# Dense products of a two-layer graph network with the weight blocks as the stationary operand

## Chip, cores and metric

One core of one Trainium2 chip. The metric is the device time of one execution in microseconds (us), the median over runs. Engines are named as the profile names them: PE (TensorE matmuls), PEld (its weight loads), DVE (VectorE), ACT (ScalarE), POOL (GpSimd), SP (SyncE, which here only issues DMAs).

## What is computed

96 nodes with 1024 features each, 1632 edges, two layers. All of it is float32. The reference, cut to what matters:

```python
h = relu(layernorm(x))                                  # 96 x 1024
q = h @ wq.T + bq;  k = h @ wk.T + bk;  v = h @ wv.T + bv
q2 = q @ wiq.T + biq;  k2 = k @ wik.T + bik;  v2 = v @ wiv.T + biv    # 16 heads of 64
attn = softmax(q2 @ k2.T / 8 + mask)                    # mask from the edges and their types
x = x + (attn @ v2) @ wo.T + bo
h = relu(layernorm(x))
u = h @ root + bias
for r in range(8):                                      # mean of h over each node's edges of type r
    u = u + mean_r(h) @ weight[r]
z = concat(u, h) @ w_gate + b_gate
x = x + tanh(u) * z + h * (1 - z)
```

That is 18 products of 96x1024 by 1024x1024: WQ, WK, WIQ, WIK, WV, WIV, WO, ROOT, eight relations and the two halves of the gate. Their weights are 72 MB and are read once.

## The kernel before

The host lays every 1024x1024 weight matrix out as four **pieces** of 1 MB: a half of the input features (four blocks of 128 on the partitions) by a half of the output features (512 columns). 72 pieces run in one fixed order.

The path of a piece: SP fetches it into one of eight slots of `raw` (L260 to L270, where slots are refilled when `split` says that the piece has been read). ACT rounds it to fp32r into `high` (`round_piece`, L413), DVE takes the rest, `raw - high`, into `low` (`split_piece`, L589); both have four slots. PE then makes, for each of the four blocks, three matmuls (`multiply`, L848 to L850): the stationary operand is a 128x96 block of the activations, high or low part, and 512 columns of the weights move past it.

```python
pe.matmul(o, stat[0][:, at], hi, start=opens and k == 0, stop=False)
pe.matmul(o, stat[1][:, at], hi, start=False, stop=False)
mm = pe.matmul(o, stat[0][:, at], lo, start=False, ...)
```

So a piece is 12 matmuls and its output has the nodes on the partitions (96x512, `acc`). The bias comes in as one more matmul for each half of a product (L861). Before such an output can be the input of the next product, it is turned: ACT copies it to `rows` (`take_rows`, L422), PE transposes four 128-wide blocks (`turn_rows`, L890) into `turn`, ACT rounds that (`take_turned`, L426), DVE takes its low part (`low_turned`, L599 or L602).

Beside the products stands the work on edges and attention: keys of the edges compared with each other (L906, L630), one-hot matrices made by POOL (L328, L354) and DVE (L648, L673), codes of the mask (L920) and counts by type (L933, 32 matmuls with 384 columns moving), scores (L950), softmax, attention transposed (L961), values mixed (L974), sums of messages (L1080, L1081) and their means (L794). Every engine's order is written out by hand; the 32 pieces of the relations run in a loop over pairs of relations (ACT, DVE and PE each have one), with the sums of the next pair inside it. The result is made by DVE (L832, L833) and stored in two halves.

Of the kernel before, what the change touches and what calls it, by code (L numbers as in the profile page):

```python
# [18 lines left out]

WQ, WK, WIQ, WIK, WV, WIV, WO, ROOT, REL0 = range(9)
PIECES = 4
RAW_SLOTS = 8  # L40
SPLIT_SLOTS = 4
# [5 lines left out]
TURNED = ["h0", "q", "k", "q2", "k2", "v", "out", "h1", "u"]  # L47

SPLIT_TURNED = ["h0", "q", "k", "v", "out", "h1", "u"]


def gnn_kernel(nc, x, weights, biases, edge_columns, edge_rows, type_weights, out):
# [4 lines left out]
    M = weights.shape[0] // PIECES  # L57
    R = M - REL0 - 2
# [9 lines left out]
    WG_X, WG_U = REL0 + R, REL0 + R + 1  # L68
    N_PIECES = PIECES * M
    FIRST_REL = PIECES * REL0  # L70
    FIRST_GATE = PIECES * WG_X
    TW = N * CH
    NB = biases.shape[0]
    LOW_ROW = 32
    ROUNDS = N_PIECES // RAW_SLOTS
    assert D == 1024 and N % 32 == 0 and N <= P and R % 2 == 0 and EC == 16 and EP <= P
    assert N_PIECES % RAW_SLOTS == 0 and FIRST_REL % RAW_SLOTS == 0

    with ExitStack() as ctx:
# [5 lines left out]


        raw = sb("raw", [P, RAW_SLOTS, CH * HALF])
        high = sb("high", [P, SPLIT_SLOTS, CH * HALF], F32R)
        low = sb("low", [P, SPLIT_SLOTS, CH * HALF], F32R)
        x_sb = sb("x_sb", [N, D])  # L90
        rows = [sb(f"rows{i}", [N, D]) for i in range(2)]
        v2 = sb("v2", [P, D])

        stat_h = [sb(f"stat_h_{s}", [P, C * N], F32R) for s in ("high", "low")]
        stat_a = [sb(f"stat_a_{s}", [P, C * N], F32R) for s in ("high", "low")]
        stat_b = [sb(f"stat_b_{s}", [P, C * N], F32R) for s in ("high", "low")]
        q2T = sb("q2T", [P, E // 2])
        k2T = sb("k2T", [P, C * N])
        attn = sb("attn", [P, E])
        attnT = sb("attnT", [P, HEADS * N])  # L100
# [3 lines left out]
        bias_rows = sb("bias_rows", [LOW_ROW + NB, D], F32R)  # L104
        bias_pick = sb("bias_pick", [LOW_ROW + NB, NB], F32R)
        bias_pick_f = sb("bias_pick_f", [LOW_ROW + NB, NB])
        per_count = sb("per_count", [P, R * N])
# [13 lines left out]
        node_iota = sb("node_iota", [EP, R * N], F16)  # L121
# [6 lines left out]
        code_m = sb("code_m", [N, 2, N])  # L128


        def inside(t, parts, first, shape, dt):

            n = int(np.prod(shape))
            flat = t[:, :] if dt == F32 else t[:, :].bitcast(dt)
# [1021 lines left out]
```

## Time and profile before

| | |
|---|---|
| median of 3 runs | 280.95 us (280.81 to 281.11) |
| span of the profiled execution | 280.8 us |
| PE, PEld busy | 247.4 us (88%), 169.8 us (60%) |
| DVE, ACT, POOL busy | 227.9 us (81%), 171.9 us (61%), 106.6 us (38%) |
| read from HBM | 76.01 MB, 272 GB/s over the span |
| chain that ended last | PE 72%, POOL 13%, DVE 9% |

The profile is one execution; its span is within 0.2 us of the median. A busy share counts the records of an engine, and the records of matmuls overlap: each lasts from its issue to the end of its way through the array. For what a matmul costs in a stream, the distance from one start to the next is read, not the mean duration. The page of the profile has the span in 40 slices; PEclk there is the granted clock of TensorE as a share of full speed (2.4 GHz; 0.5 is 1.2 GHz).

### The profile page before, as it was taken

How to read it: one execution, taken by the hardware profiler on the slowest of the kernel's cores; microseconds unless marked ns; L12 is line 12 of the kernel's file. 1: busy time of each engine (PE TensorE's matmuls, PEld its weight loads, DVE VectorE, ACT ScalarE, POOL GpSimd, SP SyncE). 2: the span in 40 equal slices, each digit the busy share in tenths (PEclk: the TensorE clock that was granted, in tenths of full speed). 3: DMA queues.
4: the chain of work that ended last, by engine and by line, in shares of the span. 5: the costliest groups of instructions: out<-in, count | busy, mean ns of one | idle time of the engine just before them, and what ended most of it. 6: DMA issues, size and time to landing. Idle time of an engine off the chain costs nothing.

```text
span 280.8 us, 3219 instructions
## 1 busy us (share of the span) xinstructions
PE 247.4 (88%) x1144; PEld 169.8 (60%) x1144; DVE 227.9 (81%) x154; ACT 171.9 (61%) x133; POOL 106.6 (38%) x79
## 2 busy tenths in 40 slices
PE   0499556999999979869589999999999999999994
PEld 0266333667666647546357667667766766666662
DVE  2599299797866979996593999999899899974992
ACT  4699703366658588635532975686686677765730
POOL 4999789593795652000100430450322044000000
PEclk9999956899999999979959999999999999999999
DMA  6999978758777764885716489999989999980001
GB/s 196 382 424 423 423 296 332 289 188 279 293 289 268 240 243 149 299 300 177 272 42 259 159 327 398 376 338 357 404 316 371 364 322 328 361 364 0 0 0 56
DMA packets 10974, 76.54 MB, mean 273 GB/s; under 512 B 1440, under 2 KB 1440, under 8 KB 1748
## 3 DMA queue, kind: packets, MB, share of 16 engines
q1 hardware_dynamic: 10964, 76.40, 72.8%
q8 instruction: 7, 0.11, 0.2%
q14 instruction: 3, 0.02, 0.0%
HBM read 76.01 MB, written 0.39 MB: 272 GB/s over the span
## 4 chain that ended last, share of the span: by engine, by line
PE 72%; POOL 13%; DVE 9%; ACT 2%; DMA 1%; issue 1%; POOLq 0%
PE acc L848 22%; PE acc L850 21%; PE acc L849 21%; POOL attn L328 7%; DVE low L589 5%; POOL attn L346 2%; PE side L933 2%; PE acc L861 2%; DVE per_count L747 1%; DMA x_sb<-in_x 1%; PE turn L890 1%; POOL edge_tmp L343 1%; PE turn L1080 1%; DVE edge_tmp L654 1%; ACT high L413 1%
## 5 line engine op out<-in xcount | busy, mean ns | idle before, releaser
L589 DVE TENSOR_TENSOR low<-raw,high 128x2048 fp32r<-128x2048 f32 x72 | 176.5, 2473 | 20.9 <-ACT high L413 20.8
L413 ACT ACTIVATE high<-raw 128x2048 fp32r<-128x2048 f32 x72 | 136.9, 1911 | 33.5 <-PE acc L850 29.5
L848 PE MATMUL acc<-high,stat_h_high 128*96 128x512 f32 x80 | 36.0, 450 | 10.9 <-DVE low L589 10.2
L848 PE MATMUL acc<-high,stat_a_high 128*96 128x512 f32 x112 | 45.1, 403 | 0.0
L850 PE MATMUL acc<-low,stat_a_high 128*96 128x512 f32 x112 | 44.2, 395 | 0.0
L849 PE MATMUL acc<-high,stat_a_low 128*96 128x512 f32 x112 | 43.9, 392 | 0.0
L848 PE MATMUL acc<-high,stat_b_high 128*96 128x512 f32 x96 | 39.0, 407 | 2.3 <-DVE stat_b_low L602 2.3
L850 PE MATMUL acc<-low,stat_b_high 128*96 128x512 f32 x96 | 38.6, 402 | 0.0
L849 PE MATMUL acc<-high,stat_b_low 128*96 128x512 f32 x96 | 38.3, 399 | 0.0
L849 PE MATMUL acc<-high,stat_h_low 128*96 128x512 f32 x80 | 34.5, 431 | 0.0
L850 PE MATMUL acc<-low,stat_h_high 128*96 128x512 f32 x80 | 34.4, 430 | 0.0
L398 POOL TENSOR_TENSOR stat_a_low<-attnT,stat_a_high 128x768 fp32r<-128x768 f32 x4 | 11.8, 2957 | 54.6 <-ACT stat_a_high L538 54.6
L848 PEld LDWEIGHTS acc<-high,stat_h_high 128*96 128x96 f32 x80 | 14.5, 182 | 18.2 <-DVE low L589 6.4
L848 PEld LDWEIGHTS acc<-high,stat_a_high 128*96 128x96 f32 x112 | 18.1, 161 | 8.3 <-issue 0.5
L850 PEld LDWEIGHTS acc<-low,stat_a_high 128*96 128x96 f32 x112 | 18.1, 161 | 7.8
L849 PEld LDWEIGHTS acc<-high,stat_a_low 128*96 128x96 f32 x112 | 18.1, 162 | 7.2
L354 POOL TENSOR_SCALAR attnT<-node_iota,edge_tmp 102x768 f16<-102x768 f16 x4 | 18.4, 4592 | 10.0 <-PE side L933 10.0
L848 PEld LDWEIGHTS acc<-high,stat_b_high 128*96 128x96 f32 x96 | 15.9, 165 | 9.1 <-DVE stat_b_low L602 2.4
L328 POOL TENSOR_SCALAR attn<-node_iota,edge_f 102x96 f16<-102x96 f16 x16 | 20.9, 1327 | 0.0
L398 POOL TENSOR_TENSOR stat_b_low<-attnT,stat_b_high 128x768 fp32r<-128x768 f32 x4 | 13.1, 3285 | 17.9 <-ACT stat_b_high L538 17.9
L850 PEld LDWEIGHTS acc<-low,stat_b_high 128*96 128x96 f32 x96 | 15.7, 164 | 6.8
L849 PEld LDWEIGHTS acc<-high,stat_b_low 128*96 128x96 f32 x96 | 15.9, 166 | 6.4
(130 smaller groups left out, 248.4 us busy)
## 6 DMA issues: line engine op xcount, KB each, us to landing
raw<-in_weights SPq DMA_DIRECT2D x72, 1024.0 KB, 6.6
x_sb<-in_x SPq DMA_DIRECT2D x1, 384.0 KB, 3.7
out<-rows SPq DMA_DIRECT2D x2, 192.0 KB, 2.1
rows<-in_biases SPq DMA_DIRECT2D x2, 36.0 KB
edge_i<-in_edge_columns SPq DMA_DIRECT2D x1, 25.5 KB
attn<-in_edge_rows SPq DMA_DIRECT2D x1, 12.8 KB
tw_in<-in_type_weights SPq DMA_DIRECT2D x1, 1.5 KB, 7.1
```

What stands on the lines that cost most here:

```text
L328: gp.tensor_scalar(src_hot[:, c, :], node_iota[:, 0:N], src_f[:, c:c + 1], None, ALU.is_equal).then_inc(src_hot_ready, 1)
L343: step(gp.tensor_scalar(zero_f, dup_f, 0.0, None, ALU.is_equal))
L346: gp.tensor_tensor(dst_hot, dst_hot, code_e.rearrange("p (c a) -> p c a", a=1).to_broadcast([EP, EC, N]), ALU.mult).then_inc(dst_hot_ready, 1)
L354: gp.tensor_scalar(rel_hot[:, c % 4, :], node_iota[:, :], rel_key_f[:, c:c + 1], None, ALU.is_equal).then_inc(rel_hot_gp, 1)
L398: gp.tensor_tensor(chunks(s[1]), mean[:, :, parity * N:(parity + 1) * N], chunks(s[0]).bitcast(F32), ALU.subtract).then_inc(mean_low, 1)
L413: act.activation(high[:, slot % SPLIT_SLOTS, :], raw[:, slot, :], ACT.Copy)\
L589: dve.tensor_tensor(low[:, s, :], raw[:, slot, :], high[:, s, :].bitcast(F32), ALU.subtract).then_inc(split, 1)
L848: pe.matmul(o, stat[0][:, at], hi, start=opens and k == 0, stop=False)
L849: pe.matmul(o, stat[1][:, at], hi, start=False, stop=False)
L850: mm = pe.matmul(o, stat[0][:, at], lo, start=False, stop=last and kind % 2 == 1 and k == CH - 1 and bias is None)
L861: return pe.matmul(acc[m % 2][0:N, b, :], bias_pick[:, m:m + 1].to_broadcast([LOW_ROW + NB, N]), bias_rows[:, b * HALF:(b + 1) * HALF], st ...
L933: mm = pe.matmul(side[0:N, b, 0:TW], src_hot[:, c, :], rel_hot[:, c % 4, b * TW:(b + 1) * TW], start=c == 0, stop=c == EC - 1)
```

## The change

Every product is turned round. The stationary operand is now a 128x128 block of the float32 weights, read from the slot into which the DMA wrote it. The activations move past it: 96 columns, one for each node, with the features on the partitions. A piece is 16 matmuls of plain float32. Its output has output features on the partitions, the form in which the next product wants it. With that:

- no `high` and `low` of weights or activations; `round_piece`, `split_piece`, `take_rows`, `take_turned`, `low_turned` are gone; 12 slots instead of 8, freed by PE itself (`piece_used`), fetched by a plain loop without a hardware loop (L256 to L262 there)
- the order of the matrices puts the gate's half that takes h (WG_X) ahead of the relations, and the order of the pieces of a matrix is first input half for both output halves, then second
- a product is taken by one DVE addition of the bias for each half (`take`, L410), the bias being per partition; no bias matmuls
- x is turned at the start (L607), the residual stays turned, v2 (L614, L682), the second layer's rows (L614) and the result (L614, L583, L584) are turned back
- one-hot matrices all on DVE, the attention's subtraction and scaling too; the counts use a table of 16 one-hot matrices and stand behind WIV and WO
- sums of messages by block of 128 features for all 8 relations (32 matmuls of 128x384 instead of 64 of 128x192), placed among the pieces of ROOT and WG_X; means of all relations are kept (24 KB per partition)

```diff
-            def multiply(n, slot, kind, stat, a, opens, last, bias=None):
-                b, k0 = kind // 2, CH * (kind % 2)
-                pe.wait_ge(split, n + 1)
-                for k in range(CH):
-                    hi = high[:, slot % SPLIT_SLOTS, k * HALF:(k + 1) * HALF]
-                    lo = low[:, slot % SPLIT_SLOTS, k * HALF:(k + 1) * HALF]
-                    at = slice((k0 + k) * N, (k0 + k + 1) * N)
-                    o = a[0:N, b, :]
-                    pe.matmul(o, stat[0][:, at], hi, start=opens and k == 0, stop=False)
-                    pe.matmul(o, stat[1][:, at], hi, start=False, stop=False)
-                    mm = pe.matmul(o, stat[0][:, at], lo, start=False,
...
+            def piece(n, moving, a, opens=True, closes=True):
+                s, kind = n % SLOTS, KINDS[n % PIECES]
+                b, k0 = kind // 2, CH * (kind % 2)
+                pe.wait_ge(raw_landed[s], 16 * (n // SLOTS + 1))
+                for c in range(CH):
+                    for k in range(CH):
+                        at = k * HALF + c * P
+                        mm = pe.matmul(a[:, b, c * N:(c + 1) * N], raw[:, s, at:at + P],
+                                       moving(k0 + k), start=opens and k0 == 0 and c == 0 and k == 0,
+                                       stop=closes and k0 > 0 and c == CH - 1 and k == CH - 1)
+                mm.then_inc(piece_used, 1)
...
-                act.activation(high[:, slot % SPLIT_SLOTS, :], raw[:, slot, :], ACT.Copy)\
-                   .then_inc(rounded, 1)
...
-                dve.tensor_tensor(low[:, s, :], raw[:, slot, :], high[:, s, :].bitcast(F32),
-                                  ALU.subtract).then_inc(split, 1)
...
+            def take(m, b, dst, bias):
+                dve.wait_ge(piece_used, done_at(m, b))
+                a = acc[1 if SEQUENCE.index(m) % 2 or m >= ROOT else 0]
+                dve.tensor_tensor(by_chunk(half(dst, b)), by_chunk(bank(a, b)), bias_of(bias, b),
+                                  ALU.add).then_inc(taken, 1)
...
+            for b in range(2):
+                pe.wait_ge(taken, taken_at(WO, b))
+                turn_columns(turn, b, xT, rows_turned)
+                for c in ((5, 6) if b == 0 else range(7, EC)):
+                    count(c)
+            pe.wait_ge(normed, 3)
+            turn_rows(turn, 0, rows, h_turned)
...
+            for r in range(R):
+                n = first_piece(REL0 + r)
+                for j in range(PIECES):
+                    if r == 0 and j % 2 == 0:
+                        pe.wait_ge(mean_ready, C if j == 0 else 2 * C)
+                    piece(n + j, of_mean(r), acc[1], opens=False, closes=r == R - 1)
```

What that makes of PE's order, first at WIQ and WIK. Before, two pieces of WIQ's 24 matmuls look so (the first rows of a piece, then the end of one with the turning of the product before it and the counts):

```order
L848 MATMUL acc<-high,stat_a_high 96x512
L849 MATMUL acc<-high,stat_a_low 96x512
L850 MATMUL acc<-low,stat_a_high 96x512
L861 MATMUL acc<-bias_rows,bias_pick 96x512
L890 MATMUL turn<-ident,rows 128x96 x4
L933 MATMUL side<-attnT,attn 96x384 x4
```

Now, WK to the first piece of WV, 16 matmuls to a piece:

```order
L596 MATMUL acc<-hT,raw 128x96 x96
L596 MATMUL acc<-qT,raw 128x96 x32
L638 MATMUL side<-dst_hot,src_hot 96x96 x8
L638 MATMUL turn<-dst_hot,src_hot 96x96 x8
L596 MATMUL acc<-qT,raw 128x96 x32
L596 MATMUL acc<-kT,raw 128x96 x64
L596 MATMUL acc<-hT,raw 128x96 x16
L659 MATMUL side<-k2T,q2T 96x96 x8
```

Three matmuls of 512 columns for a block have become four of 96 columns, nothing is turned between the products, and the counts have moved behind WIV.

PE between the layers, from WO to ROOT. Before, the end of WO, the turning of h and the first of ROOT:

```order
L850 MATMUL acc<-low,stat_b_high 96x512
L861 MATMUL acc<-bias_rows,bias_pick 96x512
L890 MATMUL turn<-ident,rows 128x96 x8
L848 MATMUL acc<-high,stat_h_high 96x512
L849 MATMUL acc<-high,stat_h_low 96x512
```

Now:

```order
L596 MATMUL acc<-hT,raw 128x96 x48
L614 MATMUL turn<-ident,xT 96x128 x4
L647 MATMUL side<-mean,src_hot 96x384 x4
L614 MATMUL turn<-ident,xT 96x128 x4
L647 MATMUL side<-mean,src_hot 96x384 x18
L607 MATMUL turn<-ident,rows 128x96 x4
L596 MATMUL acc<-hT,raw 128x96 x16
L607 MATMUL turn<-ident,rows 128x96 x4
L596 MATMUL acc<-hT,raw 128x96 x16
L798 MATMUL side<-counts,ones 128x384 x2
```

The residual's rows are turned back before the statistics, and 22 of the 32 matmuls of the counts fill the place where PE waits for the normalisation.

DVE at the end of layer 0 (WIK to WO). Before, with the low parts among the steps of the softmax:

```order
L713 SCALAR_TENSOR_TENSOR attn<-side,mask 96x384 x2
L719 TENSOR_REDUCE row_max<-attn 96x8
L589 TENSOR_TENSOR low<-raw,high 128x2048
L602 TENSOR_TENSOR stat_a_low<-turn,stat_a_high 128x384
L726 TENSOR_REDUCE row_sum<-attn 96x8
L729 RECIPROCAL row_inv<-row_sum 96x8
L589 TENSOR_TENSOR low<-raw,high 128x2048
```

Now:

```order
L512 SCALAR_TENSOR_TENSOR attn<-turn,mask 96x384 x2
L518 TENSOR_REDUCE row_max<-attn 96x8
L521 TENSOR_TENSOR attn<-attn,row_max 96x768
L410 TENSOR_TENSOR qT<-acc,bias_cols 128x384
L527 TENSOR_REDUCE row_sum<-attn 96x8
L528 RECIPROCAL row_inv<-row_sum 96x8
L530 TENSOR_TENSOR attn<-attn,row_inv 96x768
L410 TENSOR_TENSOR qT<-acc,bias_cols 128x384
```

The 72 long subtractions are gone, and two steps of the softmax have come over from POOL.

## Rows read from the trace of the kernel before

**Rows 1.** Page: span, busy times, chain that ended last.

```profile
span 280.8 us, 3219 instructions
PE 247.4 (88%) x1144; PEld 169.8 (60%) x1144; DVE 227.9 (81%) x154; ACT 171.9 (61%) x133; POOL 106.6 (38%) x79
...
PE 72%; POOL 13%; DVE 9%; ACT 2%; DMA 1%; issue 1%; POOLq 0%
```

**Rows 2.** Page: DVE's and ACT's costliest groups (line, engine, operation, count | busy, mean ns | idle before).

```profile
L589 DVE TENSOR_TENSOR low<-raw,high 128x2048 fp32r<-128x2048 f32 x72 | 176.5, 2473 | 20.9 <-ACT high L413 20.8
L413 ACT ACTIVATE high<-raw 128x2048 fp32r<-128x2048 f32 x72 | 136.9, 1911 | 33.5 <-PE acc L850 29.5
```

**Rows 3.** Timeline, PE: successive matmuls of a piece (start us, duration us, what).

```profile
68.30 0.40 PE L850 MATMUL acc<-low,stat_a_high 128*96 128x512 f32 x1
68.53 0.39 PE L848 MATMUL acc<-high,stat_a_high 128*96 128x512 f32 x1
```

**Rows 4.** Windows: stretch, engines' busy us and counts, granted clock, DMA share, GB/s.

```profile
20.00:30.00 10.00, 9.76 (x43) 6.21 (x42) 8.56 (x6) 9.92 (x10) 10.00 (x7) 1.00 1.01 423
...
130.00:140.00 10.00, 6.76 (x31) 4.42 (x32) 7.13 (x9) 5.80 (x4) 0.76 (x2) 1.00 0.62 221
```

**Rows 5.** Timeline, PE's weight loads of the message sums (128 columns), second and last.

```profile
150.10 0.19 PEld L1081 LDWEIGHTS turn<-counts,msgs_low 96*128 96x128 f32 x1
...
151.67 0.19 PEld L1081 LDWEIGHTS side<-counts,msgs_low 96*128 96x128 f32 x1
```

**Rows 6.** Timeline, PE: the matmuls of these sums (192 columns), second and last.

```profile
150.19 0.28 PE L1081 MATMUL turn<-counts,msgs_low 96*128 96x192 f32 x1
...
151.76 0.28 PE L1081 MATMUL side<-counts,msgs_low 96*128 96x192 f32 x1
```

**Rows 7.** One line's instructions, L950 (scores): loads and matmuls, min/median/max ns.

```profile
L950 PEld LDWEIGHTS side<-k2T,q2T x32: 156/162/162, 90.2 to 94.8; 64*96 64x96 f32 x32
L950 PE MATMUL side<-k2T,q2T x32: 242/245/320, 90.2 to 94.9; 64*96 64x96 f32 x32
```

**Rows 8.** Timeline, PE: the 16 records of one call of L950.

```profile
90.23 0.92 PE L950 MATMUL side<-k2T,q2T 64*96 64x96 f32 x16
```

**Rows 9.** One line's instructions: loads of L974, L1080 and L890.

```profile
L974 PEld LDWEIGHTS turn<-attnT,v x32: 133/137/137, 114.1 to 119.6; 96*64 96x64 f32 x32
...
L1080 PEld LDWEIGHTS side<-counts,msgs_high x16: 192/192/192, 150.9 to 221.4; 96*128 96x128 f32 x16
...
L890 PEld LDWEIGHTS turn<-ident,rows x64: 137/140/230, 7.6 to 261.7; 96*128 96x128 f32 x64
```

**Rows 10.** Timeline: transposes, eight at 0.5 of the clock, eight at full clock.

```profile
7.65 1.51 PE L890 MATMUL turn<-ident,rows 96*128 96x96 f32 x8 [7.65 <-DVE rows L611]
...
106.62 0.82 PE L961 MATMUL side<-ident,attn 96*96 96x96 f32 x8
```

**Rows 11.** Timeline: the start, to the first product.

```profile
8.56 0.49 ACT L426 ACTIVATE stat_h_high<-turn 128x384 fp32r<-128x384 f32 x1 [1.45 <-PE turn L890]
10.00 1.91 ACT L413 ACTIVATE high<-raw 128x2048 fp32r<-128x2048 f32 x1 [0.30 <-DMA raw<-in_weights]
14.40 0.71 PE L848 MATMUL acc<-high,stat_h_high 128*96 128x512 f32 x1 [3.71 <-DVE low L589]
...
17.74 0.39 PE L850 MATMUL acc<-low,stat_h_high 128*96 128x512 f32 x1
```

**Rows 12.** Chain that ended last in time: four matmuls of the counts (start us, us, what).

```profile
59.63 0.65 PE side L933 x4
```

**Rows 13.** Timeline: between the layers, last statistics and normalisation.

```profile
136.88 0.69 DVE L767 BATCH_NORM_STATS2 stats<-x_sb 96x6 f32<-96x512 f32 x1
...
138.76 1.00 DVE L611 TENSOR_SCALAR rows<-x_sb,moments 96x512 f32<-96x512 f32 x2 [0.95 <-POOL moments L300]
```

**Rows 14.** Timeline, the end: last product, two DVE steps, store.

```profile
276.83 0.69 DVE L832 TENSOR_TENSOR v<-acc,v 96x512 f32<-96x512 f32 x1 [2.36 <-PE acc L850]
...
278.26 0.34 SPq L273 DMA_DIRECT2D out<-rows  x1
```

More of the change, by code:

```diff
@@ L575, in _ @@
+            for b in range(2):
+                act.wait_ge(out_turned, b + 1)
+                act.activation(cols(out_rows, b), turn[0:N, b, :], ACT.Copy).then_inc(out_ready, 1)
         @block.vector
@@ L740, in _ @@
-            invert_sums(1)
+            take(WV, 0, qT, B_V)
+            divide_by_sums(0)
+            take(WV, 1, qT, B_V)
+            divide_by_sums(1)
+            take_both(WIV, kT, B_IV)
+            for b in range(2):
+                dve.wait_ge(piece_used, done_at(WO, b))
+                dve.tensor_tensor(half(xT, b), bank(acc[0], b), half(xT, b), ALU.add).then_inc(taken, 1)
+                dve.wait_ge(rows_turned, b + 1)
+                dve.bn_stats(stats[:, b, :], turn[0:N, b, :]).then_inc(vec, 1)
@@ L1015, in _ @@
[L1015 to L1030 removed]
+            piece(n + 2, of(qT), acc[0])
@@ new lines, in _ @@
+            show_scores(1)
+            piece(n + 2, of(hT), acc[0])
+            piece(n + 3, of(hT), acc[0])
+            n = first_piece(WIV)
+            pe.wait_ge(taken, taken_at(WV, 0))
+            piece(n, of(qT), acc[1])
+            turn_attn(0)
+            piece(n + 1, of(qT), acc[1])
+            pe.wait_ge(taken, taken_at(WV, 1))
+            piece(n + 2, of(qT), acc[1])
+            turn_attn(1)
+            piece(n + 3, of(qT), acc[1])
+            turn_v2(0)
+            for c in range(0, 3):
+                count(c)
@@ new lines, in _, with sum_messages @@
+            pe.wait_ge(normed, 3)
+            turn_rows(turn, 0, rows, h_turned)
+            def sum_messages(c):
+                if c == 0:
+                    pe.wait_ge(msgs_low, 2)
+                    pe.wait_ge(counts_taken, 2)
+                elif c == 1:
+                    pe.wait_ge(totals_taken, 1)
+                else:
+                    pe.wait_ge(mean_ready, 2 * (c - 1))
+                for s in range(2):
+                    for b in range(2):
+                        mm = pe.matmul(bank((turn, side)[c % 2], b), msgs[s][:, c * P:(c + 1) * P], half(counts, b),
+                                       start=s == 0, stop=s == 1)
+                mm.then_inc(sums_shown, 1)
@@ L1066, in _ @@
-            pe.wait_ge(turn_low, low_at("h1", 0))
-            piece(28, stat_h, False)
-            def sum_messages(pair):
-                if isinstance(pair, int) and pair == 0:
-                    pe.wait_ge(msgs_low, 2)
-                else:
-                    pe.wait_ge(mean_ready, pair * 2)
-                pair_counts = counts[:, bass.ds(pair * (2 * N), 2 * N)]
-                for c in range(C):
-                    o = (turn, side)[c // CH][:, (c % CH) // 2, (c % 2) * 2 * N:(c % 2 + 1) * 2 * N]
-                    pe.matmul(o, msgs[0][:, c * P:(c + 1) * P], pair_counts, start=True, stop=False)
-                    mm = pe.matmul(o, msgs[1][:, c * P:(c + 1) * P], pair_counts, start=False, stop=True)
-                mm.then_inc(sums_shown, 1)
@@ L1121 @@
+            n = first_piece(WG_U)
+            for j in range(PIECES):
+                if j % 2 == 0:
+                    pe.wait_ge(taken, taken_at(TAKEN[-1], j // 2))
+                piece(n + j, of(uT), acc[0], opens=False)
+            for b in range(2):
+                pe.wait_ge(out_made, b + 1)
+                turn_columns(turn, b, outT, out_turned)
 def kernel(**inputs):
```

895 lines of the change are left out of this document (313 added, 582 removed).

## Prediction

> **What bounds it now.** I read the page first, then the groups, then PE's timeline. The page has PE busy for 88% of the span, DVE for 81%, and the chain that ended last runs through PE for 72% [rows 1]. PE's busy share doesn't say what it could do, since records of matmuls overlap. In a piece the starts are 0.23 us apart [rows 3]: 512 columns at 2.4 GHz are 0.213 us, so this is nearly full speed. 72 pieces of 12 matmuls at 0.231 us are 200 us, 2.78 a piece, against a span of 280.8. The other 80 us are waits and small work: the head, the low parts on DVE, which cost 2.47 us a piece and wait for ACT's rounding [rows 2], and in layer 0 the edges' work on POOL, 13% of the chain. The first 30 pieces take from 14.4 to 150 us, 4.5 each [rows 11, 5]; the last 42 from 152 to 277, 3.0 each [rows 6, 14]. The DMAs moved 423 GB/s while they had free slots [rows 4], 2.48 us a piece: they are not the limit. So the change may save the distance between 200 and 281 us; what it makes of the 200 decides.
>
> **What a turned product costs.** It removes the 72 roundings and 72 low parts [rows 2], the 18 bias matmuls and the turning between products. It adds 16 plain float32 matmuls a piece. One such matmul makes two records: L950 calls it 16 times and has 32 loads and 32 matmuls [rows 7]. So the pieces are 72 x 16 x 2 = 2304 pairs of load and matmul, where there were 864 pairs.
>
> The matmul of a pair: 16 of L950 with 96 columns take 0.92 us, and the last of them lasts 0.245 [rows 7, 8]. They run two by two, on the upper and lower 64 rows of the array; eight pairs, so one start every (0.92 - 0.245)/8, about 84 ns, on each half. Transposes with 96 columns of float32 agree: eight take 0.82 us [rows 10], less the last one's 0.245 and by seven that is 82 ns. That is 2 x 96 columns at 2.4 GHz (80 ns) and some 3. Hence a pair costs at least 82 ns.
>
> The load of a pair: 64 columns have records of 137 ns, 96 columns 162 [rows 7, 9], 128 columns of fp32r 192 [rows 5, 9]. They lie on one line, some 84 ns plus 0.83 ns a column. A load of 128 columns would then hold the loading path for 107 ns, longer than the matmul. The message sums show it at work: their loads are 128 columns, their matmuls 192 columns of fp32r, which are 80 ns of streaming, just as 96 columns of float32 are. Their loads start at 150.10 and, 14 later, at 151.67 [rows 5], their matmuls at 150.19 and 151.76 [rows 6]: 112 ns a pair, not 82. This is the nearest row that there is to the new pair: same load, same streaming time. What it doesn't show is plain float32 in both, 128 rows instead of 96, and more than 1.8 us of it. The bounds are 82 ns (the load hidden, as in the transposes) and 187 ns (107 + 80, nothing hidden). I take 112, since these loads lie on the line of the plain float32 ones.
>
> A piece is then 32 x 0.1117 = 3.57 us, and 72 are **257.4 us**, 57 more than the 200 of today. The DMA's 2.48 a piece stays hidden behind it, with 12 slots; if PE were at 2.7 it would still be.
>
> The Trainium skill (TensorE: Matmul & The Clock Gate, "Back-to-back issue gap") speaks for less: a sustained stream of loads and matmuls is measured there at some 81 ns a matmul for 128 columns. By it the pieces would be 2304 x 0.081, an estimated 187 us, and the change a clear gain. The row of the message sums, with 112 ns at full clock, contradicts it for 4-byte weights, and I follow the row.
>
> **The rest of the time, all on PE's path.**
> - Head: activations of the first half were ready at 8.56 + 0.49 = 9.05 us [rows 11], and no low part is waited for any more, nor a rounding of the weights. The first piece had landed at 10.0 (ACT's wait for it ends there); now it is issued second in SP's queue, not fourth. Start at 9.4, where the first product stood at 14.40. DVE's added step on x and the bias copy on ACT lie in the wait for the statistics.
> - Clock: the first product's records last 0.71 us at 14.40 and 0.39 at 17.74, some 3.2 us on [rows 11]; till then it ran at half the clock, as the eight transposes did that take 1.51 us at the start and 0.82 later [rows 10]. Half of 3.2: 1.6 us.
> - Small matmuls: counts 32 at 0.163 [rows 12], 5.2; message sums 32 with 384 columns, 0.16 and some 0.01 each, 5.5; scores and mixing 4 calls at 0.7 to 0.85, 3.0; transposes of attention 16, of v2 and of the residual 8 each, of h 8, at 0.08 to 0.11, 3.7; keys 1.0, codes 0.8, totals 0.4. Together 19.6 us.
> - Between the layers PE waits: the last statistics can begin only after the residual's second half is added (0.55) and turned back (0.43), 2.3 us after WO; from their start to the first normalised half were 1.88 + 0.5 us [rows 13], then 0.3 for the transposes, 0.5 for ACT. That is 6.2 us, of which 4.8 are PE's own small matmuls, counted above: 1.4 idle. Around the mixing of values and at the seams 0.6. Everywhere else another piece (3.6 us) lies between a result and its use; DVE's work drops from 228 us to about 50 (228 less the 176 of the low parts [rows 1, 2]; what it gains and loses beside them is about equal), and no piece waits for it. Together 2.0.
> - End: after the last matmul two DVE steps (0.55 and 0.5), four transposes, ACT's copy (0.6) and the store, which took 2.5 us from 278.26 to the span's end [rows 14]: 4.8 us with the hand-overs, where it was 4.0.
>
> Sum: 9.4 + 1.6 + 257.4 + 19.6 + 2.0 + 4.8 = 294.8 us, against a span of 280.8, which stands 0.2 under the median. **Forecast: 295 us, slower by 5%.** The time is lost in the last 42 pieces (3.57 us and the sums, where they took 3.0) and partly won back in the first 30.
>
> **Rivals.**
> - A, the load hides behind the matmul, as for the transposes, whose 128-column loads have records of only 140 ns [rows 9] and whose pairs cost 82. For it: loads do run beside matmuls everywhere in this trace. Against: plain float32 loads follow the slow line (162 ns for 96 columns, where the transposes' have 126), and the message sums. Then 2304 x 0.0825 = 190 us, and 190 + 37.4 = **227 us**. The kernel is faster than before from 105 ns a pair downwards ((280.8 - 37.4)/2304); there the sign turns. By the Trainium skill's 81 ns it would be 224.
> - B, the clock: at 112 ns a pair the array streams for 80, and if that were too little to hold full clock, pieces would cost up to twice as much, 295 + 257 = **up to 550 us**. Against: between 130 and 140 us PE made only 31 matmuls, 0.213 each, two thirds of the time at most, and the granted clock stayed at 1.00 [rows 4]; and this stream has no gaps of microseconds.
> - C, in plain float32 a load overlaps less than in fp32r, or PE's instructions (4600 of them, unrolled) come too slowly: each pair costs between 120 and 187 ns, **314 to 468 us**. Against: in L950 loads of 96 columns (80 ns) hid wholly behind 80 ns of streaming, with two pairs begun every 84 ns.
> - That the change does not do what it says is no rival: the order of the instructions shows 16 matmuls to a piece and none of the low parts.
>
> **Chances.** Forecast 0.80, A 0.11, B 0.03, C 0.06. The forecast's own range comes from 109 to 115 ns a pair (251 to 265 us) and 3 us either way for the rest: 287 to 305 us. It holds the time 8 times in 10, so the range needs nothing of the rivals. A measurement of this kernel can tell 0.2% from no change. Faster by more than that: 0.11 (A); within: 0.01, a corner of A; slower: 0.88.
>
> **What would show it.** Right: loads and matmuls of L596 start 111 to 112 ns apart, the loads' records last 190 ns, a piece is 3.57 us, the granted clock is 1.00 from about 13 us, PE has no gap over 0.5 us but the one between the layers, DMA share is about 0.7. The first piece starts by 10 us, the last matmul ends 5 us before the end. Wrong: starts 82 to 105 ns apart (A), a granted clock of 0.5 in the products (B), starts over 120 ns apart (C), or waits for `taken` or `raw_landed` between pieces.

## The result, and the profile after

The changed kernel takes **298.05 us** (median of 4 executions, 297.73 to 298.23) against 280.98 for the kernel before on the same chip (280.81 to 281.11): a ratio of 1.064, 95% interval 1.058 to 1.071. Slower, as forecast; the range of 287 to 305 us holds it. Some executions of a kernel take over 1.5% longer than its fastest: ratios leave these out, medians and ranges hold all. The profiled execution took 297.73 us with a span of 296.2.

The page, its lines on busy times, the slices of PE, DVE and of the granted clock, the chain that ended last by engine, and the two costliest groups (out<-in, rows*columns of the stationary block, operand):

```profile
span 296.2 us, 5359 instructions
...
PE 285.5 (96%) x2519; PEld 280.7 (95%) x2519; DVE 65.1 (22%) x107; ACT 19.2 (6%) x31; POOL 17.6 (6%) x41
...
PE   2999999999999999999999999999999999999994
...
DVE  3159014701670100326424200000000000000511
...
PEclk9999999999999999999999999999999999999999
...
PE 95%; DVE 1%; DMA 1%; ACT 0%; POOL 0%; issue 0%; POOLq 0%
...
L596 PEld LDWEIGHTS acc<-mean,raw 128*128 128x128 f32 x1024 | 114.5, 192 | 0.0
L596 PE MATMUL acc<-mean,raw 128*128 128x96 f32 x1024 | 114.5, 275 | 0.0
```

PE was busy for 88% of a span of 280.8 before, DVE for 81% [rows 1]. Now PE is all that counts, with 96%, and DVE has 22%. DVE's digits are 0 from slice 24 to 37, which is where the relations' products run. Both sides of PE, loads and matmuls, count as busy nearly throughout, so the busy share can't say which of the two sets the pace. The distance between starts can, and it stands in the chain. The chain that ended last in order of time (start us, us, what, how many):

```profile
8.75 5.83 PE acc L596 x32
...
15.06 3.74 PE acc L596 x32
...
19.27 28.75 PE acc L596 x256
...
98.60 3.57 PE acc L596 x32
...
135.27 3.55 PE acc L596 x32
138.82 0.74 PE turn L786 x4
...
162.40 128.62 PE acc L596 x1152
```

The last line has 36 pieces in one stretch in which PE waits for nothing: 128.62 us for 1152 pairs of load and matmul are **111.65 ns a pair**, 3.57 us a piece. One piece of the first layer (98.60) takes the same. The first piece takes 5.83, since it runs at half the clock at first.

Where the time went can be read against the kernel before. There the last 42 pieces lay from 152 to 276.8 us [rows 6, 14]; here they lie from 135.3 to 291.0. So up to their start the change gains 16.7 us, over the 42 pieces it loses 155.7 - 124.8 = 30.9, and behind the last product 1.2 more (5.2 us instead of 4.0). That makes 15.4 us more, the difference of the spans. The gain of the first part was real: low parts and roundings are no longer waited for. A second gain lies in the clock. In the trace of the kernel before, the granted clock fell to half in four stretches between 34.6 and 147.3 us, 23.9 us together. The last of them, from 140.4 to 147.3, lies in this window (stretch, engines' busy us and counts, granted clock, DMA share, GB/s):

```profile
140.00:150.00 10.00, 9.28 (x30) 5.82 (x29) 6.66 (x6) 3.84 (x5) 0.00 (x0) 0.66 0.37 138
```

Its matmuls of 512 columns start 0.43 us apart there instead of 0.23. In the changed kernel the clock is full from 13.1 us to the end, which is worth at most half of the 23.9, an estimated 12 us of the first part. The slower products cost nearly twice what the first part gained.

Between the layers (timeline, PE and DVE; in brackets the idle time before and its releaser):

```profile
122.03 0.54 DVE L544 TENSOR_TENSOR xT<-acc,xT 128x384 f32<-128x384 f32 x1
...
122.62 0.64 PE L614 MATMUL turn<-ident,xT 128*96 128x128 f32 x4 [0.59 <-DVE xT L544]
...
125.19 1.52 DVE L425 TENSOR_SCALAR rows<-turn,moments 96x512 f32<-96x512 f32 x2 [0.95 <-POOL moments L273]
...
127.18 2.02 PE L596 MATMUL acc<-hT,raw 128*128 128x96 f32 x16 [0.58 <-ACT hT L332]
```

The last product of WO ends at 120.94 by the chain, the first of ROOT starts at 127.18: 6.2 us, most of it filled with the counts.

### The profile page after: what moved, and what is told of

It is laid out like the page before. It is cut to its first block, busy times and chain, and to the rows that moved or that the text cites. A ratio compares the mean times of both kernels' runs of the same rounds, so it can differ in the third digit from the quotient of the medians.

```text
span 296.2 us, 5359 instructions
## 1 busy us (share of the span) xinstructions
PE 285.5 (96%) x2519; PEld 280.7 (95%) x2519; DVE 65.1 (22%) x107; ACT 19.2 (6%) x31; POOL 17.6 (6%) x41
## 4 chain that ended last, share of the span: by engine, by line
PE 95%; DVE 1%; DMA 1%; ACT 0%; POOL 0%; issue 0%; POOLq 0%
PE acc L596 88%; PE side L647 2%; DMA x_sb<-in_x 1%; PE turn L786 1%; PE side L786 1%; PE turn L614 1%; PE turn L607 1%; PE turn L682 1%; DVE stats L430 0%; PE side L659 0%; PE turn L659 0%; DVE stats L546 0%; PE turn L666 0%; PE side L666 0%; DVE rows L425 0%
## 5 line engine op out<-in xcount | busy, mean ns | idle before, releaser
L596 PEld LDWEIGHTS acc<-mean,raw 128*128 128x128 f32 x1024 | 114.5, 192 | 0.0
L596 PE MATMUL acc<-mean,raw 128*128 128x96 f32 x1024 | 114.5, 275 | 0.0
L596 PEld LDWEIGHTS acc<-hT,raw 128*128 128x128 f32 x768 | 89.4, 196 | 2.1 <-ACT hT L332 1.0
L596 PE MATMUL acc<-hT,raw 128*128 128x96 f32 x768 | 90.9, 279 | 0.6 <-ACT hT L332 0.6
L596 PE MATMUL acc<-qT,raw 128*128 128x96 f32 x256 | 29.4, 275 | 0.0
L596 PEld LDWEIGHTS acc<-qT,raw 128*128 128x128 f32 x256 | 29.0, 192 | 0.0
L410 DVE TENSOR_TENSOR uT<-acc,bias_cols 128x384 f32<-128x384 f32 x2 | 1.1, 558 | 111.6 <-PE acc L596 111.6
L596 PE MATMUL acc<-kT,raw 128*128 128x96 f32 x128 | 14.5, 275 | 0.0
L596 PE MATMUL acc<-uT,raw 128*128 128x96 f32 x128 | 14.5, 275 | 0.0
L596 PEld LDWEIGHTS acc<-uT,raw 128*128 128x128 f32 x128 | 14.4, 192 | 0.0
L596 PEld LDWEIGHTS acc<-kT,raw 128*128 128x128 f32 x128 | 14.4, 192 | 0.0
L410 DVE TENSOR_TENSOR kT<-acc,bias_cols 128x384 f32<-128x384 f32 x4 | 2.2, 558 | 22.9 <-PE acc L596 22.9
L607 PE MATMUL side<-ident,x_sb 96*128 96x96 f32 x8 | 1.5, 371 | 4.1 <-DMA x_sb<-in_x 4.1
L607 PEld LDWEIGHTS side<-ident,x_sb 96*128 96x128 f32 x8 | 1.3, 224 | 4.1 <-issue 4.1
```

The costliest lines, as they stand in the source:

```text
L410: dve.tensor_tensor(by_chunk(half(dst, b)), by_chunk(bank(a, b)), bias_of(bias, b), ALU.add).then_inc(taken, 1)
L596: mm = pe.matmul(a[:, b, c * N:(c + 1) * N], raw[:, s, at:at + P], moving(k0 + k), start=opens and k0 == 0 and c == 0 and k == 0, stop=clo ...
L607: t = pe.transpose(dst[:, b, c * N:(c + 1) * N], src[:, (b * CH + c) * P:(b * CH + c + 1) * P], ident[0:N, 0:N])
```

## The experiments

The theory (T) is the one of the prediction: a pair costs the longer of two things, the load of the stationary columns (0.83 ns each) and the streaming of the moving ones (two clock periods each, in plain float32), and a few ns more. The rivals differ from run to run and are named in the expectations. The kernel before ran beside them each time, on the same chip as they did, with medians of 278.24 to 281.15 us. Spans are those of the profiled execution. Where a kernel takes columns out, DVE zeroes the accumulators once at the start.

### Fewer columns loaded

```diff
-                        mm = pe.matmul(a[:, b, c * N:(c + 1) * N], raw[:, s, at:at + P],
+                        mm = pe.matmul(a[0:96, b, c * N:(c + 1) * N], raw[:, s, at:at + 96],
```

> The products load only 96 of each block's 128 columns (32 output features of each 128 are left out and stay zero; DVE zeroes both accumulators at the start); the matmuls move the same 96 columns. Theory T (a pair of load and matmul lasts as long as the longer of the two, and the load of 128 columns, 107 ns, is the longer): the load falls to 80 ns, a pair to 84, 2304 pairs to 194 us, the time from 298 to about 235 us. Rival S (the stream of the matmul, four passes over the activations, sets the 112 ns, or something per instruction does): 112 ns stays, 298 us. Rival H (the pair is the matmul and a third of the load, 80 + 0.3 x 107): 104 ns, 280 us.

Measured: 236.34 us, span 234.8. First the same 36 pieces in the chain, then one line's loads (count: duration in ns min/median/max, first and last start; the last count is of a sample):

```profile
131.71 97.93 PE acc L599 x1152
```

```profile
L599 PEld LDWEIGHTS acc<-mean,raw x1024: 161/165/165, 131.4 to 218.4; 128*96 128x96 f32 x171
```

97.93 us for 1152 pairs are 85.0 ns a pair. A quarter of the loaded columns less takes 26.7 ns off each pair, though the matmuls move what they moved. That is 0.83 ns a column: the load set the pace. At 96 and 96 both sides of T come to 80 ns, so the 85 don't tell which of them is the longer here; they are 80 and 5.

### Fewer columns moved

```diff
-                        mm = pe.matmul(a[:, b, c * N:(c + 1) * N], raw[:, s, at:at + P],
-                                       moving(k0 + k), start=opens and k0 == 0 and c == 0 and k == 0,
+                        mm = pe.matmul(a[:, b, c * N:c * N + 64], raw[:, s, at:at + P],
+                                       moving(k0 + k)[:, 0:64], start=opens and k0 == 0 and c == 0 and k == 0,
```

> The products move 64 of the 96 columns (nodes 64 to 95 are left out of all products; DVE zeroes the accumulators); the loads keep 128 columns. Theory T: the load is still 107 ns, so a pair stays at 112 ns and the time at 298 us, within 1. Rival S (stream): the matmul falls from 80 to 53 ns, a pair to about 85, the time to 236 us. Rival H (matmul and a third of the load): 53 + 32 = 85 ns, too.

Measured: 380.08 us, span 378.6. None of the theories had this. The chain in order of time:

```profile
24.63 54.81 PE acc L599 x256
...
138.61 20.67 PE acc L599 x96
...
187.32 0.78 PE side L650 x4
188.10 3.59 PE acc L599 x32
...
244.78 128.60 PE acc L599 x1152
```

Up to 187 us a pair takes 54.81/256 = 214 ns, behind it 128.60/1152 = 111.6. That is a factor of 1.92: the clock. Up to there TensorE ran at 1.2 GHz, though it hardly paused; the first change of the granted clock that this trace records lies at 187.2 us, upwards. Before that came products of this form for 178 us, with short groups of small matmuls among them; what stands directly ahead of the rise, from 182.2 us on, are transposes, counts (L650) and the mixing of values. The windows of the same trace (stretch, engines' busy us and counts, granted clock, DMA share, GB/s) show how this misleads:

```profile
20.00:120.00 100.00, 100.00 (x477) 99.28 (x477) 21.01 (x35) 0.00 (x0) 11.62 (x15) 1.00 0.57 217
...
200.00:300.00 100.00, 98.83 (x856) 97.35 (x854) 19.72 (x32) 3.58 (x7) 0.76 (x2) 1.00 0.72 256
```

Both read 1.00, with 477 and 856 matmuls in the same time. The profile takes the clock from its changes, and ahead of the first one its 1.00 is not a measurement.

Two things follow. At full clock a pair with 64 moving columns costs what one with 96 costs, 111.6 ns: the load sets the pace and T holds, while any theory in which load and matmul add up would have given less. And rival B of the prediction, to which I gave 0.03, has a mechanism that exists: in this run the clock stayed at its low level for 178 us of products. In the changed kernel it rose at 13.1 us. It is one execution of the kernel with 64 columns; whether the columns decide between the two, or whether another execution would rise early, was not tested.

### More columns moved

```diff
+            def twice(t):
+                return t.rearrange("p (a n) -> p a n", a=1).to_broadcast([P, 2, N])
...
-                        mm = pe.matmul(a[:, b, c * N:(c + 1) * N], raw[:, s, at:at + P],
-                                       moving(k0 + k), start=opens and k0 == 0 and c == 0 and k == 0,
+                        mm = pe.matmul(a[:, b, (c % 2) * 2 * N:(c % 2 + 1) * 2 * N], raw[:, s, at:at + P],
+                                       twice(moving(k0 + k)), start=opens and k0 == 0 and c == 0 and k == 0,
```

> The products move the same 96 columns twice (192 columns, 160 ns of streaming; two blocks of outputs are summed on top of each other, so the numbers are another computation's); the loads keep 128 columns. Theory T: now the matmul is the longer one and hides the load: a pair is 160 + 3 to 5, 164 ns, 2304 pairs 378 us, the time about 418 us. Rival H (matmul and a third of the load): 192 ns, 483 us. With nothing hidden it would be 267 ns, 655 us.

Measured: 415.2 us, span 413.7. One line's matmuls (columns as above), with 166.2 us between the first and the last start, for 1023 steps:

```profile
L599 PE MATMUL acc<-mean,raw x1024: 323/326/326, 221.1 to 387.3; 128*128 128x192 f32 x171
```

That is 162.5 ns a pair: 192 columns by two periods are 160, and 2.5. The same load of 128 columns costs nothing here. So load and matmul do overlap wholly, and 111.7 in the changed kernel is not the sum of parts of both. The Trainium skill (TensorE: Matmul & The Clock Gate, "Part 3: Packing small matmuls — row/col tiling") says that a load overlaps a running matmul only where the two use different row groups. Here each load and each matmul use all 128 rows, and the trace shows them overlapping: with nothing overlapped it would be 107 + 160.

### Not turned round, but plain float32 all the same

```diff
-                for c in range(CH):
-                    for k in range(CH):
-                        at = k * HALF + c * P
-                        mm = pe.matmul(a[:, b, c * N:(c + 1) * N], raw[:, s, at:at + P],
...
+                for k in range(CH):
+                    mm = pe.matmul(a[0:N, b, :], moving(k0 + k), raw[:, s, k * HALF:(k + 1) * HALF],
```

> The changed kernel with only the direction of its products turned back: the activations (96 columns) are the stationary operand, all 512 columns of the weights in plain float32 move past them, 4 matmuls a piece instead of 16 and no weight split. The output then has the wrong form for the steps after it, so those work on other numbers (DVE zeroes the accumulators at the start). Theory T: a record streams 2 x 512 columns, 427 ns, its load of 80 ns is hidden: 8 records by 430 to 445 ns, 3.44 to 3.56 us a piece instead of 3.57; the time 288 to 298 us. So it is plain float32, four passes where the split has three, that costs the 0.7 us a piece over the kernel before, and the turning round by itself costs nearly nothing. Rival S (the turned form's own overhead is what costs): below 3.0 us a piece, 257 us or less.

Measured: 287.66 us, span 286.2, at the lower edge of what T gave. The windows (columns as above) count the PE records of 20 us in the relations:

```profile
180.00:200.00 20.00, 20.00 (x48) 7.59 (x47) 0.00 (x0) 0.00 (x0) 0.00 (x0) 1.00 0.86 308
```

48 records of 512 columns, some of them cut by the window's edges, 20 us / 48 = 0.42; from first to last start of the group with `mean` (157.2 to 266.6, 255 steps) it is 0.429 us a record, 8 of them 3.43 us a piece. So most of what the products lost doesn't come from turning them: with the activations stationary, plain float32 costs 3.43 us where three products of fp32r took 2.78, and turning it round adds 0.14 more, 10 us over 72 pieces. The 10.4 us between the two kernels' times (298.05 and 287.66) are these.

### Two halves of 64 columns, side by side in the array

```diff
-                        mm = pe.matmul(a[:, b, c * N:(c + 1) * N], raw[:, s, at:at + P],
-                                       moving(k0 + k), start=opens and k0 == 0 and c == 0 and k == 0,
-                                       stop=closes and k0 > 0 and c == CH - 1 and k == CH - 1)
+                        for g in range(0, P, 64):
+                            mm = pe.matmul(a[g:g + 64, b, c * N:(c + 1) * N], raw[:, s, at + g:at + g + 64],
+                                           moving(k0 + k), start=opens and k0 == 0 and c == 0 and k == 0,
+                                           stop=closes and k0 > 0 and c == CH - 1 and k == CH - 1)
```

> The whole computation, but each 128x128 block is used as two stationary blocks of 64 columns, the second on the other half of the array's columns (output partitions 64 to 127), so twice as many pairs, 4608. Theory T with what the mixing of values (two 64-column blocks at a time) shows: both halves load 64 columns (53 ns) and stream 96 (80 ns) beside each other, two pairs in 82 to 84 ns, the products 189 to 194 us instead of 257, the time 230 to 236 us: faster than both kernels. Rival L (loads of the two halves pass one after the other): 2 x 53 + 5 = 112 ns for two pairs, 298 us, no change. Rival I (PE can't take up instructions that fast for long: 4 in 82 ns): between 112 and 250 ns for two pairs, 300 us or more.

Measured: 244.73 us (6 executions, 241.62 to 247.59), 0.868 of the kernel before (0.861 to 0.875), and not the 230 to 236 that T gave. It computes all that the reference does. Three views follow: PE's timeline within the relations; the waits of PE's weight loads (engine, tile, line, releaser: us in all, times, longest); the DMA queues on the page (packets, MB, share of 16 engines):

```profile
183.80 4.04 PE L597 MATMUL acc<-mean,raw 128*64 128x96 f32 x93
188.54 5.50 PE L597 MATMUL acc<-mean,raw 128*64 128x96 f32 x128 [0.70 <-issue]
194.73 5.50 PE L597 MATMUL acc<-mean,raw 128*64 128x96 f32 x128 [0.70 <-issue]
```

```profile
PEld acc L597 <- issue: 13.4, 24, 1.1
```

```profile
q1 hardware_dynamic: 10704, 76.09, 79.8%
q8 instruction: 37, 0.61, 1.0%
```

128 matmuls take 5.50 us, of which the last one's record is 0.25 (5.25/128): 41 ns each, 82 for the two halves of what was one pair of 111.7. By T's 0.83 ns a column two loads of 64 columns one after the other would take 107 ns. So they stand beside each other and beside the matmuls, and the streaming alone sets the pace: T's price for the products was right. What it left out are stops. Of the 24 waits above, 8 are gaps of 0.25 to 0.31 us where a piece follows small matmuls of another form; the changed kernel has two such gaps as well. The other 16 lie inside the products, 0.2 to 1.1 us each and 11.3 us together, most of them after 127 or 128 matmuls and as many loads, and what PE then waits for is "issue", nothing that the profile shows. 37 packets of instructions with 0.61 MB are about 16.5 KB each (16384 bytes in the trace), about one for each 256 of the 9967 instructions. These packets end the stops. In the trace, three of them begin at 186.17, 192.27 and 199.01 us and last 0.97, 1.02 and 0.95; PE goes on at 188.54, 194.73 and 201.20, that is 1.4, 1.4 and 1.2 us after they end. In all 56 such stops, of this run and of the runs below that split the block in the same way, PE goes on 1.2 to 1.6 us after a packet of instructions has ended. In the changed kernel there are 20 such packets and no stops; there 256 instructions last 14 us, here 5.3. The Trainium skill (Runtime: NRT & Kernel Launch, "Instruction fetch mechanics") says that instructions come in blocks of 16 KiB for 256 of them and that this is mostly hidden. The size agrees. That it is hidden holds for the changed kernel and not for this one.

### What the stops hang on

Half of each piece's bytes from the 13th piece on, everything else as in the two halves (the products with the rest use what lay in the slot):

```diff
-                sp.dma_start(raw[:, n % SLOTS, :], weights[where]).then_inc(raw_landed[n % SLOTS], 16)
+                w = CH * HALF if n < SLOTS else CH * HALF // 2
+                sp.dma_start(raw[:, n % SLOTS, 0:w], weights[where][:, 0:w]).then_inc(raw_landed[n % SLOTS], 16)
```

> The two-halves kernel (col64), which took 245 instead of the 231 us that its 82 ns for two pairs give, with only the first half of each piece fetched from the 13th piece on (the other half of a slot keeps old weights). Theory F (PE runs out of instructions: it stands still for some 0.9 us after every 128 matmul records, 24 times, 13 us together, since a fetch of 16 KB of instructions shares the DMA engines with weights that keep them 95% busy): with the weights' traffic halved the stops shrink to nearly nothing, 231 to 234 us. Rival G (the fetch itself is too slow for four instructions in 82 ns, whatever else the DMAs do): the stops stay, 240 us or more. Rival W (PE waits for weights): they go as well, but then they'd stand in the trace as waits for DMAs, which col64 has not.

Measured: 236.6 us, span 235.1. PE's timeline over the same stretch as above, and PEld's waits for issue:

```profile
183.75 16.42 PE L598 MATMUL acc<-mean,raw 128*64 128x96 f32 x394
```

```profile
PEld acc L598 <- issue: 4.4, 12, 1.0
```

The same instructions and as many packets of them (38 and 37), but no stop at all in the relations. Behind the 8 gaps of the seams 4 stops are left, 2.3 us, between 30 and 50 us, when weights still arrived at over 400 GB/s. The time is above the 231 to 234 us expected, and these stops are most of the difference. So it is not the instructions' number alone: their packets come late where the weights' transfers occupy the DMA engines. But busy DMA engines alone do not make a stop. With all bytes (the kernel of the two halves) the first of these windows has no stop and the second has six (columns as above):

```profile
140.00:180.00 40.00, 40.00 (x976) 40.00 (x972) 1.83 (x4) 0.00 (x0) 0.00 (x0) 1.00 0.97 373
182.00:213.00 31.00, 27.96 (x652) 27.02 (x649) 0.00 (x0) 0.00 (x0) 0.00 (x0) 1.00 0.90 340
```

What sets a stop off within such a stretch stays open.

Then the transfers' form: two of 4 KB rows for each piece instead of one of 8 KB.

```diff
-                sp.dma_start(raw[:, n % SLOTS, :], weights[where]).then_inc(raw_landed[n % SLOTS], 16)
+                for h in range(2):
+                    w = slice(h * CH * HALF // 2, (h + 1) * CH * HALF // 2)
+                    sp.dma_start(raw[:, n % SLOTS, w], weights[where][:, w]).then_inc(raw_landed[n % SLOTS], 16)
```

> col64 with each piece fetched by two transfers of 4 KB rows instead of one of 8 KB rows, the whole computation. The stops of PE in col64 differ by steps of 0.27 us, the time of one 8 KB packet. Theory F with queueing (a fetch of instructions waits behind packets of weights already handed to its DMA engine): packets of half the size let it through earlier, the stops of 0.9 us shrink to 0.5 or less, 234 to 240 us. Rival (the wait goes by bytes or by time, not by packets): the stops stay, 242 to 246 us. If the smaller rows cost bandwidth, PE will wait for weights: over 246 us.

Measured: 248.42 us (246.92 to 250.34), 0.892 of before (0.883 to 0.901); `PEld acc L599 <- issue` has 12.6 us in 21 waits, the longest 2.2; 13 of them, 10.5 us, are stops within the products. A miss: the 234 to 240 us of the expectation did not come, and smaller rows did not let the instructions through earlier.

And how many transfers are queued at once, by the number of slots (`SLOTS = 12` in the change):

> col64 with 6 slots for weights instead of 12, the whole computation. The DMAs then work off fewer pieces ahead of PE and are idle more evenly. Theory F with queueing: fetches of instructions find the engines free more often in the first 80 us, where the DMAs of the 12-slot kernel run at 420 GB/s without a break, so part of the stops goes there: 238 to 244 us. Rival: the stops stay the same, or PE now waits for weights at the seams, 245 us or more.

> col64 with 4 slots, the whole computation. With 12 slots the DMAs run 12 pieces ahead, with 6 the median was 243. Theory F with queueing: with 4 slots there are never more than 3 pieces queued, the engines have pauses from the start, and the stops in the first 60 us go; those of the relations stay, as there the DMAs follow PE piece by piece in each version: 240 to 244 us. Rival: with 3 pieces (7.9 us) ahead PE waits for weights after each seam: 247 us or more.

> The kernel of col64_s4 once more on another occasion, for an interval beside the kernel before. Its profile had 233.7 us and hardly a stop of PE for instructions, its other executions 235 to 241. Theory F (few queued weights, few stops): the ratio to the kernel before lies at 0.84 to 0.87, the time at 234 to 240 us. Rival (that profile was luck, the stops come back): as col64_s6, 243 us, 0.865 to 0.88.

> The same with 3 slots: only 2 pieces are queued while PE works on one. A piece landed 4.7 to 5.1 us after its issue in the runs with more slots, twice PE's 2.62 us is 5.2. If the 5 us are mostly queueing behind the other pieces (2.5 us is the transfer), 3 slots suffice: 233 to 240 us. If they are latency, PE waits for weights at most pieces: 245 us or more.

| slots | us, median (lowest to highest), executions | PEld's wait for "issue" in the profiled one: us, times, longest | of it stops within the products: us, times |
|---|---|---|---|
| 12 | 244.73 (241.62 to 247.59), 6 | 13.4, 24, 1.1 | 11.3, 16 |
| 6 | 243.24 (237.59 to 244.30), 4 | 12.0, 21, 1.4 | 9.9, 13 |
| 4 | 237.42 (235.19 to 241.39), 4 | 2.7, 9, 0.6 | 0.6, 1 |
| 4, again | 238.74 (233.78 to 241.68), 6 | 8.7, 16, 1.7 | 6.6, 8 |
| 3 | 246.36 (246.25 to 247.35), 4 | 4.3, 12, 0.9 | 0.2, 1 |

From 4 slots (span 233.7) to 4 again, 6 and 12 (240.2, 242.7, 244.5) the spans grow by 6.5, 9.0 and 10.8 us and the waits by 6.0, 9.3 and 10.7: the stops make up the differences. With 3 slots three more of the 12 waits stand at the start of a piece.

Six slots met their expectation, also in where the stops went: 3 of 13 lie ahead of 60 us, where 12 slots have 6 of 16. Four slots were better than the 240 to 244 expected. The repetition gives 0.850 of before over the medians of all its executions (238.74 to 280.98), inside the 0.84 to 0.87 expected. The six times are 233.8, 233.9, 236.8, 240.7, 240.9 and 241.7 us; the profiled one of the first group was of the lower kind and has no stop in the relations, the profiled one of the second was of the upper kind and has eight, from 186 us on. Why they come in one execution and not in another stays open. With three slots the result is the one expected for a wait on latency (245 us or more), though PE's loads wait for weights at 14 of the 72 pieces and not at most of them (waits, same columns):

```profile
PEld acc L597 <- DMA raw<-in_weights: 8.8, 14, 1.1
```

That bounds the matter from below: with three slots, so two pieces queued while PE works on the third, the weights come late. From above the bound is soft: with 6 and 12 slots the medians are 4 to 7 us higher than with 4, but the ranges of 4 and of 6 overlap, and with 4 the stops came back in some executions. A hardware loop over the relations, which would need fewer instructions, was not tried.

### The small transfers on SP's queue

```diff
+            sp.dma_start(cols(x_sb, 1), cols(x, 1)).then_inc(x_landed[1], 16)
+            sp.dma_start(bias_rows[:, :], biases.rearrange("m (c p) -> (m c) p", p=P)).then_inc(bias_landed, 16)
...
-            act.dma_start(cols(x_sb, 1), cols(x, 1)).then_inc(x_landed[1], 16)
-            act.dma_start(bias_rows[:, :], biases.rearrange("m (c p) -> (m c) p", p=P)).then_inc(bias_landed, 16)
```

> The changed kernel with its five small transfers on SP's queue instead of ACT's, ahead of the weights. In the runs so far the time stands 1.5 us above the span wherever ACT's queue is used, and 0.2 above it in the kernel before. If the second queue costs that, the distance between time and span falls from 1.5 to about 0.2 us; if it is something else of the program (its unrolled length, say), it stays at 1.5. The span itself grows by up to 1.5 us, as the first piece is issued behind six transfers.

Measured: 300.29 us, span 298.5, so 1.8 us still lie outside the span and ACT's queue has nothing to do with them. The first product moved from 8.69 to 9.93 (timeline, PE):

```profile
9.93 1.35 PE L596 MATMUL acc<-hT,raw 128*128 128x96 f32 x5 [1.70 <-DMA raw<-in_weights]
```

With the weights issued seventh on their queue they land later than the statistics. That is the other half of the head's term: in the changed kernel they stand second there, and the first product waits for ACT, not for them. The span grew by 2.3 us, more than the 1.5 expected. The first product starts 1.2 us later, and the first piece takes 7.11 us instead of 5.83, since the clock rose at 16.9 us here and at 13.1 there: with the later start the low clock lasted 7.0 us of the products and not 4.4.

## Why the prediction was right

By its terms, the profiled execution beside it (19 stretches of L596 in the chain, with 2304 pairs and 260.5 us together):

| term | forecast | trace |
|---|---|---|
| head, to the first product | 9.4 | 8.75 |
| first pieces at half the clock | 1.6 | 5.83 - 3.57 = 2.3 |
| 72 pieces | 257.4 | 260.5 - 2.3 = 258.2 |
| small matmuls and waits | 19.6 + 2.0 | 291.02 - 8.75 - 260.5 = 21.8, of it 1.8 not on PE |
| end | 4.8 | 5.2 |
| sum | 294.8 | 296.2 |

- **The pair.** This term decided, and it stood on one row, the message sums' 112 ns [rows 5, 6]. In the trace after it is 111.65. Its reading was right as well, and the experiments carry it: 128 loaded columns set the pace at 64 and at 96 moving ones, 96 loaded ones bring the pair down to 85.0, where both sides are equal, and at 192 moving ones the load is free (162.5). The Trainium skill (TensorE: Matmul & The Clock Gate, "Back-to-back issue gap") has some 81 ns a matmul for a sustained stream at 128 columns; the trace does not agree. Its section "LDWEIGHTS (loading the stationary operand)", which counts P/1.2 ns for P columns, would give an estimated 107 ns for 128 of them, and with the few ns for each pair the trace agrees.
- **The seams.** 258.2 instead of 257.4: behind the groups of L627, L659 and L607 the next piece takes 3.74 to 3.81 instead of 3.57, behind the message sums 3.54. I had not priced that.
- **The clock.** 2.3 instead of 1.6 us. I took half of 3.2 us from the old kernel; the new one starts earlier and the clock rose at 13.1 us, as forecast ("about 13 us"), so it ran longer at the low level. In this trace the head's 0.65 us and this term cancel: what starts earlier starts at half speed. It is no rule, as with the small transfers on SP's queue the first product started 1.2 us later and the clock rose 3.8 us later.
- **Waits.** Between the layers 6.2 us, as forecast, but in part by luck. The steps that the prediction names for it add up to 5.5 (2.3 + 1.88 + 0.5 + 0.3 + 0.5). In the trace they take 2.36 + 1.89 + 0.85 + 0.58 + 0.55. No piece waited for `taken` or `raw_landed`. DVE has 65 us and not "about 50"; nothing waits for them.
- **The last 1.5 us.** The sum is 1.4 us under the span, and the span 1.5 under the execution's own time. In the runs made later the kernel before shows that gap too (282.1 us with a span of 280.4); I had set its span of 280.8 beside a median of 280.95 and read the gap as nothing; the time of the execution that was profiled for it is not on record. The gap is in every kernel here, 1.5 to 1.9 us in the profiled executions.
- **The range.** Its lower end doesn't come out of its own terms: 251 + 37.4 - 3 is 285, not 287. The measured time is far from that end.
- **Rivals.** A (the load hidden, 227 us) fell. What the transposes had [rows 9, 10], loads of 128 float32 columns with records of 140 ns, these loads don't have: 192 ns. Its size could be reached, though, in another way: with two halves of 64 columns the pair costs the 82 ns that A had. C (120 ns and more) fell; its second half, instructions that come too slowly, did appear at twice the rate of instructions. B didn't happen with 96 columns and did with 64. Its 0.03 was priced on too little: the stretch from 130 to 140 us, with PE two thirds busy and the clock full, ends 0.4 us before the clock fell to half, and the same trace has three falls more. That argument was also about how a high clock is kept, and in the run with 64 columns the question was how a low one is left. So that B stayed away is luck as far as its reasons go.

## What to carry to other kernels

Before matmuls are turned round or weights kept in float32, count pairs of load and matmul and price each at the longer side: here 0.83 ns for each loaded column against two periods for each moved one, plus 2 to 5 ns; at 128 loaded and 96 moved the load is the longer, and busy shares of 95% on both sides don't tell which it is. If the load is, split the stationary block over two column halves of the array, so that loads stand beside one another (here 298 to 245 us, and 237 to 239 with four slots), and then look for stops of "issue" within the products, at even counts of instructions, while the DMAs are full. Compare spans with spans, and read the clock from distances between starts until the profile has recorded its first change.

## What the hardware showed that I had not expected

- The run with 64 moved columns stayed at 1.2 GHz up to 187 us (214 ns a pair) and went on at 111.6 ns behind the rise; the profile's clock row reads full speed all the while.
- PE's instructions arrive in packets of 16 KB. At 256 instructions in 5.3 us and with weights arriving at 340 to 420 GB/s they stopped PE for 0.2 to 1.1 us, 16 times in 37 packets, and each time PE went on 1.2 to 1.6 us after a packet had ended; at 256 in 14 us they never did. With four slots for weights there were fewer stops; with smaller rows the time did not fall.
- In the run with 4 KB rows the granted clock fell to half at the end of a stop of 2.1 us (at 196.04 us), for 3.4 us.
- Loads overlapped matmuls wholly, with all rows in use by both: 162.5 ns for a pair whose parts take 107 and 160.
